# Reordering the first 20 microseconds of a recurrent-plus-gated-MLP kernel: one more tile folded from plain fp32 factors, other load and split orders

## The reference, cut to what matters

```
h1 = xn (w1 + 2 B1 A1)^T          # 512 -> 1376, rank 16
h3 = xn (w3 + 2 B3 A3)^T
g  = silu(h1) * h3
out = x + conv(xn, K) * silu(g (w2 + 2 B2 A2)^T)   # 1376 -> 512
```

## Time and profile before

| | |
|---|---|
| median of 3 runs | 417.64 us |
| the runs | 418.46, 417.64, 417.42 us |
| profiled execution: its time, its span | 418.46 us, 416.7 us |
| PE busy | 409.2 us, 98% |
| PEld / DVE / ACT / POOL busy | 341.0 / 160.8 / 102.7 / 66.9 us |
| granted TensorE clock, every slice | 1.00 |
| critical chain by engine | PE 93%, DVE 2%, DMA 2%, SP's queue 1%, issue 1% |
| DMA | 26.15 MB in 14191 packets, 63 GB/s mean |

### The profile page before, as it was taken

The page is one execution under the profiler, slowest core; times in us unless marked ns, Lnnn a source line. Parts: engine busy times, 40 slices in busy tenths (PEclk is TensorE's granted clock), DMA queues, the critical chain, the costliest instruction groups (busy, mean ns, idle before and its releaser), DMA issues.

```text
span 416.7 us, 5035 instructions
## 1 busy us (share of the span) xinstructions
PE 409.2 (98%) x1867; PEld 341.0 (82%) x1867; DVE 160.8 (39%) x251; ACT 102.7 (25%) x168; POOL 66.9 (16%) x132
## 2 busy tenths in 40 slices
PE   8999999999999999999999999999999999999995
PEld 8978888887888888888888888888888888888883
DVE  5777776664592321242234231224124111111115
ACT  7554332323241111222121111112112111111111
POOL 5236527224400114000000103300000000000000
PEclk9999999999999999999999999999999999999999
DMA  8656733220525101000015101000002000000002
GB/s 281 162 200 173 281 79 93 77 76 19 152 77 177 52 0 51 2 0 0 2 43 201 60 0 51 0 0 0 0 0 100 0 0 0 0 0 0 0 0 101
DMA packets 14191, 26.15 MB, mean 63 GB/s; under 512 B 2544, under 2 KB 4336, under 8 KB 14176
## 3 DMA queue, kind: packets, MB, share of 16 engines
q1 hardware_dynamic: 13728, 24.85, 18.7%
q0 software_dynamic: 160, 0.59, 0.4%
q10 hardware_dynamic: 288, 0.52, 0.4%
HBM read 20.33 MB, written 4.53 MB: 60 GB/s over the span
## 4 chain that ended last, share of the span: by engine, by line
PE 93%; DVE 2%; DMA 2%; SPq 1%; issue 1%; ACT 0%; POOL 0%; DVEq 0%; ACTq 0%; POOLq 0%
PE h L831 20%; PE h L832 20%; PE h L833 20%; PE f L832 9%; PE f L831 9%; PE f L833 9%; DMA lora_stack<-lora_spread_split 2%; PE spare L818 1%; PE h L847 1%; SPq L491 1%; PE spare L813 1%; DVE w L667 1%; DVE gate L722 1%; PE spare L832 0%; PE spare L833 0%
## 5 line engine op out<-in xcount | busy, mean ns | idle before, releaser
L831 PE MATMUL h<-xt,w 128*128 (+2 forms) x356 | 137.8, 387 | 0.2 <-DVE w L667 0.2
L832 PE MATMUL h<-xt,w 128*128 (+2 forms) x356 | 137.4, 386 | 0.0
L833 PE MATMUL h<-xt,w 128*128 (+2 forms) x356 | 137.3, 386 | 0.0
L709 DVE TENSOR_TENSOR g<-g,h 128x512 f32<-128x512 f32 x44 | 30.3, 688 | 125.7 <-PE h L833 125.7
L831 PEld LDWEIGHTS h<-xt,w 128*128 128x128 f32 x356 | 66.9, 188 | 13.8 <-DVE w L667 0.6
L833 PEld LDWEIGHTS h<-xt,w 128*128 128x128 f32 x356 | 66.9, 188 | 13.4
L832 PEld LDWEIGHTS h<-xt,w 128*128 128x128 f32 x356 | 66.9, 188 | 13.1
L714 DVE TENSOR_TENSOR ghl<-g,ghl 128x512 fp32r<-128x512 f32 x44 | 31.9, 726 | 99.0 <-ACT ghl L559 99.0
L559 ACT CAST ghl<-g 128x512 fp32r<-128x512 f32 x44 | 27.3, 621 | 168.1 <-PE f L833 157.3
L831 PE MATMUL f<-ghl,w2f 128*128 128x512 f32 x176 | 68.6, 390 | 0.0
L832 PE MATMUL f<-ghl,w2f 128*128 128x512 f32 x176 | 68.5, 389 | 0.0
(11 more groups left out here) (109 smaller groups left out, 271.7 us busy)
## 6 DMA issues: line engine op xcount, KB each, us to landing
raw<-w_dram SPq DMA_DIRECT2D x28, 256.0 KB, 3.4
xres<-xT_dram SPq DMA_DIRECT2D x4, 1024.0 KB, 7.1
outT_dram<-xres SPq DMA_DIRECT2D x16, 256.0 KB, 2.4
rows_next<-x_dram SPq DMA_DIRECT2D x4, 512.0 KB, 3.6
scale_rows<-scales_scratch SPq DMA_DIRECT2D x3, 512.0 KB, 3.9
rows<-x_dram SPq DMA_DIRECT2D x2, 512.0 KB, 7.4
raw<-w_dram SPq DMA_DIRECT2D x4, 224.0 KB, 2.5
lora_stack<-lora_spread_split SPq DMA_DIRECT2D x3, 204.0 KB, 4.1
```

The lines of the kernel that those rows point to most:

```text
L709: nc.vector.tensor_tensor(g[:, :], g[:, :], h3[:, :], ALU.mult).then_inc(g_done, 1)
L831: pe.matmul(out, w[1], m[0], start=start, stop=False)
L832: pe.matmul(out, w[0], m[1], start=False, stop=False)
L833: return pe.matmul(out, w[0], m[0], start=False, stop=stop)
```

## The change

Seven edits, all in the preparation:

1. (2,0) becomes a plain tile. Its factors (128 columns of A2, 512 of B2) join `lr`, which grows from 1536 to 2176 columns, and its fold moves from the "gate" of tile 1 into `start`. The wait for the stack moves with it from (2,0) to the next fold in order, (1,2), which is placed at the same "gate".
2. VectorE clears 1216 instead of 832 columns of `lr`, GpSimd 960 instead of 704.
3. SP issues raw (1,0) before it waits for the clearing.
4. SP issues `trig` and raw (2,1) before it waits for `spread_lo`, instead of behind the stack copies. One semaphore covers `trig` and the two small state-space loads.
5. VectorE does both `rows_lo(0)` and `rows_lo(1)` before `spread_lo`, the adds of (1,1) and (3,1) before `rows_lo(2)`, and the add and subtraction of (2,0) at the end of the prologue. ScalarE does `rows_hi(0)`, `rows_hi(1)` and `fold_hi(3,0)` before `spread_hi`.
6. TensorE: one transpose group is done between the plain folds, and the groups 2 and 3 come after the first product's second part; the fold of (2,0) stands between two product groups.
7. B = Vc Bp is two fp32 matmuls of one column with 64 used partitions in place of one matmul of two columns with 128.

```
-FIRST_COLS = {1: 2 * D, 3: 2 * D + 2 * P}
-LORA_FIRST = 2 * D + 4 * P
+FIRST_COLS = {1: 2 * D, 3: 2 * D + 2 * P, 2: 2 * D + 5 * P}
+LORA_FIRST = 3 * D + 5 * P
-FACTORS_BY_DVE = 832
-PLAIN = {1: 1, 3: 1, 2: -1}
+FACTORS_BY_DVE = 1216
+PLAIN = {1: 1, 3: 1, 2: 0}
+FOLD_FIRST = [(1, 0), (3, 0), (1, 1), (3, 1), (2, 0)]
...
-        return {"gate": [(2, 0), (1, 2)], "up": [(3, 2), (1, 3)], ...
+        return {"gate": [(1, 2)], "up": [(3, 2), (1, 3)], ...
...  SP
             load_tile(0)
+            load_raw(1, 0)
             sync.wait_ge(factors_dve, 1)
...
-            load_raw(1, 0)
...
             sync.dma_start(vc_sb[:, :], s4_vc).then_inc(bvec_in, 16)
+            sync.dma_start(trig_sb...).then_inc(s4_in, 16)
+            load_raw(2, 1)
             sync.wait_ge(spread_lo, 1)
... the six stack copies, then
-            early = [(1, 2), (3, 2), trig, (1, 3), (2, 1), (3, 3)], dft
+            early = [(1, 2), (3, 2), (1, 3), (3, 3)], dft
...  ScalarE
             rows_norm(1)
+            rows_hi(0)
             fold_hi(1, 0)
-            rows_hi(0)
+            rows_hi(1)
+            fold_hi(3, 0)
             act.wait_ge(spread_in, 32)
             (spread_hi)
             rows_norm(2)
-            rows_hi(1)
             rows_norm(3)
-            fold_hi(3, 0)
             rows_hi(2)
+            fold_hi(1, 1)
             rows_hi(3)
-            fold_hi(1, 1)
             fold_hi(3, 1)
+            fold_hi(2, 0)
             hidden(0, 0)
...  VectorE
             fold_add(3, 0)
+            rows_lo(0)
             fold_lo(1, 0)
-            rows_lo(0)
+            rows_lo(1)
             dve.wait_ge(spread_hi, 1)
             (spread_lo)
-            rows_lo(1)
             fold_lo(3, 0)
+            fold_add(1, 1)
+            fold_add(3, 1)
             rows_lo(2)
             rows_lo(3)
-            fold_add(1, 1)
-            fold_add(3, 1)
             fold_lo(1, 1)
             fold_lo(3, 1)
+            fold_add(2, 0)
+            fold_lo(2, 0)
             hidden_mul(0, 0)
...  TensorE
-                if (kind, j) == FOLDS[len(FOLD_FIRST)]:
+                if (kind, j) == (1, PLAIN[1] + 1):
                     pe.wait_ge(stack_in, 2 * len(STACK) * 16)
...
                 fold(1, 0)
-                fold(3, 0)
                 pe.wait_ge(const_in, 16)
                 turn_rows(0)
+                fold(3, 0)
+                turn_rows(1)
                 fold(1, 1)
-                turn_rows(1)
-                fold(3, 1)
-                turn_rows(2)
                 (four matmuls, high by high)
-                turn_rows(3)
+                fold(3, 1)
                 (waits; eight matmuls, high by low)
+                turn_rows(2)
+                turn_rows(3)
                 hidden(0, 0, 0, 3, h3, lo)
+                fold(2, 0)
                 pe.wait_ge(xlo_done, RT)
                 hidden(0, 0, 0, 1, h1, hi)
-                pe.matmul(bankt[:, 0:2], vc_sb[:, :], bp_sb[:, :], ...)
+                for ri in range(2):
+                    mm = pe.matmul(bankt[:, ri:ri + 1], vc_sb[:, ri * P:(ri + 1) * P], bp_sb[:, :], ...)
```

More of the change, by code:

```diff
@@ L120 @@
 STACK_STEP = P // R
-FACTORS_BY_DVE = 832
-PLAIN = {1: 1, 3: 1, 2: -1}
-A_FIRST = {1: 0, 3: D}
-FOLD_FIRST = [(1, 0), (3, 0), (1, 1), (3, 1)]
+FACTORS_BY_DVE = 1216
+PLAIN = {1: 1, 3: 1, 2: 0}
+A_FIRST = {1: 0, 3: D, 2: 2 * D + 4 * P}
+FOLD_FIRST = [(1, 0), (3, 0), (1, 1), (3, 1), (2, 0)]
 def folds(place, j):
@@ L135, in folds @@
     if j == 1:
-        return {"gate": [(2, 0), (1, 2)], "up": [(3, 2), (1, 3)], "down": [(2, 1), (3, 3)]}[place]
+        return {"gate": [(1, 2)], "up": [(3, 2), (1, 3)], "down": [(2, 1), (3, 3)]}[place]
     if place == "down":
@@ L256, in build @@
         scales = put("scales", [P, 2, RT])
-        bp_sb = put("bp_sb", [P, 2])
+        bp_sb = put("bp_sb", [NS, 1])
         scal = put("scal", [P, 2])
@@ L285, in build @@
         even_odd = put("even_odd", [P, 2, D // 2])
-        vc_sb = put("vc_sb", [P, P])
+        vc_sb = put("vc_sb", [NS, 2 * P])
         krow = put("krow", [P, P + D])
@@ L322, in build @@
         spread_in, stack_in, stack_cleared = sem("spread_in"), sem("stack_in"), sem("stack_cleared")
-        s4_in, trig_in, bvec_in, dft_in = sem("s4_in"), sem("trig_in"), sem("bvec_in"), sem("dft_in")
+        s4_in, bvec_in, dft_in = sem("s4_in"), sem("bvec_in"), sem("dft_in")
         res0_in, res_in = sem("res0_in"), sem("res_in")
@@ L478, in _ @@
             sync.dma_start(spread[:, LANES_ST:LANES_ST + LANES_MV], lora_mv).then_inc(spread_in, 16)
-            for kind, j in FOLD_FIRST[2:] + [(2, 0)]:
+            for kind, j in FOLD_FIRST[2:]:
                 load_raw(kind, j)
@@ L484, in _ @@
             sync.dma_start(vc_sb[:, :], s4_vc).then_inc(bvec_in, 16)
+            sync.dma_start(trig_sb[:, :, :].rearrange("p a l -> p (a l)"), trig.to_broadcast([P, 2 * D])) \
+                .then_inc(s4_in, 16)
+            load_raw(2, 1)
             sync.wait_ge(spread_lo, 1)
@@ L492, in _ @@
                                    spread_hl[:, hl, lane_cols].bitcast(F32)).then_inc(stack_in, 16)
[L493 to L498, removed]
+            early = [(1, 2), (3, 2), (1, 3), (3, 3)]
+            for kind, j in early:
                 load_raw(kind, j)
             sync.dma_start(dft_sb[:, :, :], dft).then_inc(dft_in, 16)
-            later = [f_ for f_ in FOLDS[len(FOLD_FIRST):] if f_ not in early + [(2, 0)]]
+            later = [f_ for f_ in FOLDS[len(FOLD_FIRST):] if f_ not in early + [(2, 1)]]
             for kind, j in later[:6]:
@@ L587, in body @@
                         if first and (j, place) == (1, "gate"):
-                            act.wait_ge(trig_in, 16)
+                            act.wait_ge(s4_in, 16 * 3)
                             act.wait_ge(small_ready, 1)
@@ L880, in start @@
                 pe.wait_ge(bvec_in, 32)
-                pe.matmul(bankt[:, 0:2], vc_sb[:, :], bp_sb[:, :], start=True, stop=True).then_inc(b_ready, 1)
+                for ri in range(2):
+                    mm = pe.matmul(bankt[:, ri:ri + 1], vc_sb[:, ri * P:(ri + 1) * P], bp_sb[:, :], start=True, stop=True)
+                mm.then_inc(b_ready, 1)
                 hidden(0, 0, 0, 3, h3, hi).then_inc(h3_ready, 1)
@@ L1042, in fold_lo @@
                 pool.wait_ge(wlo_pool, POOL_LO.index((kind, j)) + 1)
-            pool.wait_ge(s4_in, 16 * 2)
+            pool.wait_ge(s4_in, 16 * 3)
             then(ts(small[:, MINUS_LOG_STEP:MINUS_LOG_STEP + 1], scal[:, 1:2], -1.0, ALU.mult))
@@ L1179 @@
                          twice(p[:, 0]), twice(p[:, 1])], axis=1)
-    vct = vc.transpose(2, 1, 0).reshape(2 * NS, NS)
-    vct = _np.concatenate([vct, vct], axis=1)
-    bp = _np.asarray(L0_attn_Bp)
-    no = _np.zeros_like(bp)
-    bp = _np.concatenate([_np.concatenate([bp, no]), _np.concatenate([no, bp])], axis=1)
+    vct = vc.transpose(1, 2, 0)
+    vct = _np.concatenate([vct[:, 0], vct[:, 0], vct[:, 1], vct[:, 1]], axis=1)
     a1, b1, a3, b3, a2, b2 = (_np.asarray(a) for a in (L0_ffn_lora_A1, L0_ffn_lora_B1, L0_ffn_lora_A3,
@@ L1192 @@
         "w1": c(turned_tiles(L0_ffn_w1)), "w3": c(turned_tiles(L0_ffn_w3)), "w2": c(_np.asarray(L0_ffn_w2).T),
-        "lora": _np.concatenate([a1, a3, b1.T[:, :2 * P], b3.T[:, :2 * P]], axis=1),
+        "lora": _np.concatenate([a1, a3, b1.T[:, :2 * P], b3.T[:, :2 * P], a2[:, :P], b2.T], axis=1),
         "lora_st": lora_st.reshape(P, LANES_ST),
         "lora_mv": lora_mv.reshape(P, LANES_MV),
-        "s4_lanes": c(lanes_d), "s4_vc": c(vct), "s4_bp": c(bp),
+        "s4_lanes": c(lanes_d), "s4_vc": c(vct), "s4_bp": c(_np.asarray(L0_attn_Bp)),
         "s4_scalars": c(_np.stack([_np.asarray(L0_attn_D), _np.asarray(L0_attn_log_step)], axis=1)),
```

## The result

The change made the kernel slower: 419.93 us (419.90 to 420.11) against 417.72 us (417.42 to 418.46), 4 runs each; the ratio is 1.0051, 95% interval 1.0034 to 1.0068. Forecast were 418.1 and "no change", with 419.4 as the upper end. The profiled execution took 420.03 us with a span of 418.2 us; so 1.8 us lie around the span, as before.

The account below looks back on a forecast made before the run. TensorE's dense stream was taken as the bound, VectorE setting part of its prologue. Terms -0.75 + 0.88 + 0.86 + 0.1 + 0.23 - 0.63 - 0.23 = +0.46 gave 418.1 against the median 417.64; range 417.1 to 419.4.

Parts of the forecast that it names:

- finish line: First matmul of h3 of tile 1, ending the prologue; the some 394 us behind it were taken as the same stream.
- The prediction's own sign of being wrong: A changed span behind the first matmul of h3 of tile 1, where times should agree within 0.3 us.
- Rival C: VectorE slips beside GpSimd's four small operations near 13 us; one loss of 0.49 makes +0.95, 418.6; 10%.
- first product's second part: In the prologue, TensorE continues at 12.6 instead of 13.35 because VectorE's second `rows_lo` ends earlier: a gain of 0.75.
- fp32 fold of (2,0): TensorE's plain fold in the prologue, two instructions of 512 columns at 0.43: +0.86, bounds 0.23 and 0.89.
- B in two products: Four small fp32 instructions on TensorE in place of two, starting 0.114 apart: +0.23, bounds 0 and 0.46.
- stall at the stack: TensorE's wait of 0.63 (21.67 to 22.30) for the stack copies goes, because TensorE comes later: -0.63.
- fold of (2,0) at the gate: The fp32r fold that the plain fold replaces leaves the gate of tile 1: -0.23 of TensorE's time.
- B (the stack becomes the wall): Last stack copy lands late, at 24.35 if it takes a quarter more, and TensorE waits: +1.8, 419.4; 14%.
- D: Faster: the (2,0) fold costs 0.23 to 0.5 in the prologue, B is free: -0.3, 417.0 to 417.4; 15%.
- E: Start of TensorE's fast stretch moves, slow spacing lasting some 3 us longer: +1.5 to +2, 419.4; 5%.
- The wait of the Silu of tile 0: ScalarE ends this Silu at 19.9, TensorE needs it at 20.2: hidden, with 0.3 to spare.

Follow-up runs that it names:

- early_lo: The changed kernel with VectorE's subtraction for the low part of (1,2) moved ahead of the product of tile 1; 419.24 us.
- pool_late: The changed kernel with one memset of 384 columns added on GpSimd ahead of den_im; 418.90 us.
- before_delay: The kernel before with two fp32 products of 128 columns added on TensorE behind the folds at the gate of tile 1; 419.46 us.
- before_delay_pool: The kernel before with two fp32 products added on TensorE at the gate of tile 1 and a 384-column memset on GpSimd ahead of den_im; 418.09 us.
- no_plain2: The changed kernel with edits 1 and 2 undone, so (2,0) is folded from the stack at the gate of tile 1 again; 419.04 us.
- before_again: The kernel before, unchanged, run again for a second profile; 417.78 us, profiled execution 418.02.
- b_one: The changed kernel with edit 7 alone undone: B is one fp32 product of two columns with 128 used partitions again; 419.59 us.
- no_plain2_rows: The changed kernel with edits 1 and 2 undone, and rows 2 and 3 ahead of the adds of (1,1) and (3,1) on VectorE, rounding likewise on ScalarE; 418.42 us.

## Why the prediction was wrong, step by step

**"All that is behind the finish line is the same stream in both kernels, except one short fold that leaves before it": wrong, +1.04.** This is the step that failed. That the fold of (2,0) leaves the gate was priced at -0.23, TensorE's time alone. But VectorE's add and ScalarE's rounding of (2,0) left the gate with it, and these had stood ahead of the add of (1,2), of ScalarE's den operations and so of GpSimd's den_im. The add of (1,2) starts 0.27 behind F in place of 0.79, den_im 3.55 in place of 4.07; the subtraction of (1,2) waits behind the product that needs h3 of tile 1 and stays near 3.7 behind F. So den_im, 0.37 to 0.40 behind the subtraction in the two traces of before, is 0.11 ahead of it, and L went from 9.69 to 10.73. early_lo, pool_late, before_delay and before_delay_pool show that the loss is the meeting of these two; no_plain2 shows that it goes when (2,0) is back at the gate. The prediction's own sign of being wrong, a span behind the finish line changed by over 0.3, came true. Rival C had the mechanism, from the earlier trace rows, and looked for it at 13 us, where the four small operations of GpSimd in fact ran from 15.35 on and lengthened none of VectorE's. Its price of 0.49 was from a case in which VectorE started 0.42 into an instruction of 1.04; the subtraction that starts 0.1 behind an instruction of 1.30 loses 1.06. The Trainium skill ("SBUF — State Buffer", section "SBUF: two separate sides") has a rule for it: VectorE with two SBUF inputs and a GpSimd instruction that reads SBUF hold the shared port pair for a whole instruction each, and the second one waits. The traces agree in who waits: 1.73 to 1.76 for VectorE as the second, 1.43 to 1.47 against 1.28 to 1.30 for GpSimd as the second, and the memset, which reads nothing, lengthened nothing. In size both lose some 0.13 less than the rest of the other's instruction (1.06 of 1.19 at 27.16, 0.17 of 0.31 at 27.07). The sentence on this page in the prediction, that such a meeting would cost less than 0.49, was about the small operations and holds for these only.

**The baseline: wrong by 0.46.** The working was against the profile's 418.46 and its F of 23.00, and came out right there (+0.46 forecast, +0.50 measured). That is luck: that profile was itself 0.46 late, and the terms fell short by 0.49 (below). The result was then put on the median of 417.64 unchanged. But 0.46 of the 0.8 between that execution and the median lay in the prologue, before the finish line (before_again: F 22.54). The changed kernel does not have these 0.46 to win: against a usual execution its F is 0.96 later. 0.96 + 1.04 = 2.00 is the difference of the two profiled times, 418.02 and 420.03; the medians differ by 2.2.

**The terms**, each against before_again:

```
step                               forecast   measured
first product's second part        -0.75      -0.66   (13.05 -> 12.39)
two transposes behind it           +0.88      +0.79   (13.29 -> 14.20, less 0.12)
fp32 fold of (2,0)                 +0.86      +0.95   (15.59 -> 16.66, less 0.12)
wait for rows 3, restarts          +0.10      +0.18
B in two products                  +0.23      +0.47   (b_one)
stall at the stack                 -0.63      -0.46   (21.37 -> 21.83)
fold of (2,0) at the gate          -0.23      -0.32   (0.71 -> 0.39)
sum                                +0.46      +0.95
```

The first row: `rows_lo(1)` ended 0.8 earlier relative to the first add, as worked out, and the add came at 7.52. The load of `lr` took 4.0 in place of 3.4 and TensorE waited 0.9 for it, at the late end of what I had allowed for; most of it was hidden, since VectorE's statistics end at 7.39 anyway. (The load grew by 40 KB, from 96.0 to 136.0, not by the 43 of the working; that changes nothing.) B was priced by the pace of eight equal instructions in a row, not by what a small product costs between two others. What in edit 7 costs the 0.47 (one column, 64 used partitions, two pairs of instructions) no run separates.

**"The fold of (2,0) is 0.86 on the path": right as a sum, misleading as a cause.** Without it F is later, not earlier (no_plain2). TensorE and VectorE met near 16.65, close to the 16.8 worked out, so neither one's cost could be taken off alone; the cost of edit 5's second half was hidden behind the fold, and the fold's behind edit 5. no_plain2_rows shows the size of the hidden part: 0.82 in F, 0.65 of it behind the first add, and 0.62 in the medians.

**The rivals.** B (the stack becomes the wall) did not come about: the last copy landed near 21.6, well ahead of 23.1. D and E did not either. The wait of the Silu of tile 0 stayed hidden (18.96 to 19.55, needed at 20.36).

## What to carry to other kernels

Two engines that share a port and are driven by different chains (here VectorE behind TensorE, GpSimd behind ScalarE) make time a step function of their phase: before taking an operation out of one chain, or delaying one by a few tenths, list in the trace which instruction of the one starts within a microsecond of which of the other, and what the loser frees. An operation that moves takes its work on every engine along, and what stood behind it there starts earlier. Price a change against several executions of the kernel before, term by term, and put a working made on one profile on a median only after knowing where that profile's own surplus lies. Where two engines arrive together, undoing one engine's addition need not show its cost; test both.

## What was not expected of the hardware

A memset of 384 columns on GpSimd beside VectorE's subtraction left it at 0.68 us, while an addition of two SBUF tensors made it 1.74. Adding this 0.42 us instruction made the program 1.0 us (changed kernel) and 1.4 us (delayed kernel before) faster. Two fp32 products of one column (64 used partitions) cost TensorE 0.47 us more than one product of two columns (128 partitions), though the same columns went through. The pace of TensorE's first instructions changes at a different time from execution to execution, with the same granted clock of 1.00 in the windows: the 22 dummy instructions at the start took 5.06 us in the first trace of the kernel before, 4.15 in the second, and 4.35 in that of the changed kernel.
